# Plain fp32 gates in the first four pairs, row copies on ScalarE, and one-hot products inside a shared step, in a mixture-of-experts feed-forward kernel

## What is computed

```
y = einsum('bct,bcd->bdt', x, weights[conditions])        # 1024 tokens x 256
probs = softmax(y @ w_router); top_w, top_i = top_k(probs, 4)   # weights normalised to sum 1
g = silu(y @ we1[e]) * (y @ we3[e])                        # per chosen expert, hidden width 128
moe = sum over the four of top_w * (g @ we2[e])
shared = silu(y @ ws1) * (y @ ws3) @ ws2                   # hidden width 512
out = x + shared / 5 + moe * 4 / 5
```

## Time and profile before

| what | value |
|---|---|
| median of three runs | 180.62 us (178.18 to 182.24) |
| the profiled execution | 178.29 us |
| its span, first to last instruction | 176.5 us |
| mean granted TensorE clock | 0.934 of full speed |
| busy: TensorE, VectorE, ScalarE, GpSimd | 78%, 69%, 43%, 39% of the span |
| HBM read and written | 17.58 MB, 6.42 MB |

### The profile page before, as it was taken

The page is one execution under the profiler, slowest core; times in us unless marked ns, Lnnn a source line. Parts: engine busy times, 40 slices in busy tenths (PEclk is TensorE's granted clock), DMA queues, the critical chain, the costliest instruction groups (busy, mean ns, idle before and its releaser), DMA issues.

```text
span 176.5 us, 3102 instructions
## 1 busy us (share of the span) xinstructions
PE 137.0 (78%) x903; PEld 119.5 (68%) x903; DVE 122.0 (69%) x286; ACT 76.6 (43%) x168; POOL 69.0 (39%) x79
## 2 busy tenths in 40 slices
PE   5956979389862068739997999699999989697950
PEld 2416658178652058629987999699999978586930
DVE  3203688697889757843778786888887752677992
ACT  3004857945375055713483667464344411322000
POOL 1500000000677877777720055576766664200000
PEclk9999999979999558985899999999999999999996
DMA  3545889700399975697661235354453222289733
GB/s 93 184 102 127 248 260 298 240 4 0 85 266 303 335 213 146 185 281 227 163 184 61 92 135 195 119 194 166 179 207 127 91 90 88 45 257 385 300 106 132
DMA packets 29952, 30.50 MB, mean 173 GB/s; under 512 B 4688, under 2 KB 26832, under 8 KB 29936
## 3 DMA queue, kind: packets, MB, share of 16 engines
q1 hardware_dynamic: 22976, 19.41, 34.1%
q0 software_dynamic: 3120, 8.52, 14.9%
q10 hardware_dynamic: 3840, 2.38, 4.4%
HBM read 17.58 MB, written 6.42 MB: 136 GB/s over the span
## 4 chain that ended last, share of the span: by engine, by line
PE 49%; DVE 18%; DMA 10%; SPq 6%; ACT 6%; issue 6%; ACTq 2%; DVEq 1%
PE up_ps L927 17%; PE down_ps L945 9%; PE gate_ps L903 6%; PE gate_ps L854 5%; DVE acc L326 4%; DMA w_raw<-store_t 4%; PE up_ps L854 3%; DVE w_lo L577 3%; PE down_ps L869 3%; SPq L355 3%; PE down_ps L913 2%; DMA g<-in_L_cond_weights,cond_idx 2%; ACT g_hi L494 2%; DVE store_t L759 2%; DVE acc L722 2%
## 5 line engine op out<-in xcount | busy, mean ns | idle before, releaser
L419 POOL DMA_INDIRECT store_t<-y_of,token_i x32 | 35.0, 1094 | 47.4 <-DVE token_i L692 38.0
L426 POOL DMA_INDIRECT result<-store_t,back_i x32 | 31.1, 973 | 30.7 <-DVE store_t L759 26.1
L759 DVE SCALAR_TENSOR_TENSOR store_t<-down_ps,valid,store_t 128x256 f32 x47 | 22.7, 483 | 9.7 <-DVE store_t L759 5.2
L903 PE MATMUL gate_ps<-ident,w_raw 128*128 128x128 f32 x94 | 16.1, 299 | 12.0 <-DMA w_raw<-store_t 12.0
L903 PEld LDWEIGHTS gate_ps<-ident,w_raw 128*128 128x128 f32 x94 | 12.1, 154 | 12.8 <-issue 8.1
L522 ACT ACTIVATE g_hi<-down_ps 128x256 fp32r<-128x256 f32 (+1 forms) x24 | 9.1, 379 | 26.5 <-PE down_ps L913 26.5
L945 PE MATMUL down_ps<-w_hi,g_hi 128*128 x47 | 14.2, 303 | 5.0 <-DVE g_lo L735 5.0
L577 DVE TENSOR_TENSOR w_lo<-w_raw,w_hi 128x768 fp32r<-128x768 f32 x10 | 9.4, 953 | 10.0 <-ACT w_hi L453 9.9
L869 PE MATMUL down_ps<-w_hi,g_hi 128*128 128x256 f32 x32 | 9.5, 298 | 8.5 <-DVE g_lo L600 8.5
L530 ACT ACTIVATE sil<-up_ps 128x256 f32<-128x256 f32 (+1 forms) x24 | 9.1, 380 | 15.2 <-PE up_ps L927 15.2
L927 PE MATMUL up_ps<-w_hi,g_hi 128*128 x48 | 15.2, 316 | 0.0
(11 more groups left out here) (160 smaller groups left out, 369.5 us busy)
## 6 DMA issues: line engine op xcount, KB each, us to landing
w_raw<-store_t SPq DMA_DIRECT2D x48, 128.0 KB
w_lo<-result SPq DMA_DIRECT2D x8, 512.0 KB, 8.5
store_t<-in_L_ffn_we SPq DMA_DIRECT2D x30, 128.0 KB, 3.3
w_raw<-in_L_ffn_we SPq DMA_DIRECT2D x18, 128.0 KB, 3.6
w_raw<-in_L_ffn_ws SPq DMA_DIRECT2D x12, 128.0 KB, 2.7
acc<-in_x SPq DMA_DIRECT2D x2, 512.0 KB, 4.9
y_of<-store_t ACTq DMA_DIRECT2D x1, 1024.0 KB, 8.5
out<-acc ACTq DMA_DIRECT2D x8, 128.0 KB, 1.8
```

The source lines that it names most:

```text
L419: pool.indirect_dma_start(xs[:, j, :], None, y_of, bass.IndirectOffsetOnAxis(ap=token_i[:, j:j + 1], axis=0),).then_inc(tile_in[j % TT], 16)
L426: pool.indirect_dma_start(result, bass.IndirectOffsetOnAxis(ap=back_i[:, j:j + 1], axis=0), merged[:, j, :], None,).then_inc(result_out[j ...
L759: dve.scalar_tensor_tensor(out=into, in0=out_ps[n % 2][:, h, :], scalar=valid[:, it:it + 1], in1=into, op0=ALU.mult, op1=ALU.add).then_inc ...
L903: last = pe.transpose(xt_ps[b][:, h, k * P:(k + 1) * P], xt[:, r, h, k * P:(k + 1) * P], ident[:, :])
```

## The change

1. **Layouts.** Unit buffers hold gate and up only (128x512). All 13 early raw buffers stay resident, so loads wait for nothing up to the loop (SP goes from 178 rows to 28 in the program); down weights `w_2` come in bigger loads of their own and are used as plain fp32. Rows and weights are read in an order that makes pieces in DRAM twice as long.
2. **Down products in plain fp32** (shared and experts): one matmul in place of three, no high and low part of the gated product. ScalarE only copies the turned product (`gt`).
3. **Gates of pairs 0 to 3 in plain fp32** from the raw weights (`PLAIN = 4`): they need no split. From pair 4 on three fp32r matmuls per product as before.
4. **Row copies by ScalarE**, two pairs ahead (`AHEAD = 2`), no longer by DMAs of the SP queue. Gathers on GpSimd from the ninth on wait until TensorE has turned enough pairs (`LEAD = 6`).
5. **Router**: logits come out untransposed, 32 small matmuls in place of 8 large ones, a copy and 8 transposes.
6. **One-hot products** stand between the gate half and the up half of shared step 2; `row_hot` is made by 32 small VectorE instructions (`tensor_scalar`) in place of 4 large ones (`tensor_tensor`); the item table's arithmetic stands behind the products.
7. **Clearing**: 8 result tiles by ScalarE before the loop, the other 24 by VectorE memsets, two tiles each, in rounds 4 to 15.
8. **The end**: ScalarE weights the rows of tiles 0 to 3, VectorE adds them for two tiles at once, combines tiles 4 and 5 itself, and TensorE takes tiles 6 and 7. Stores go by two tiles on SP, the last on ScalarE's queue.

```diff
-    RAW = 4
+    PLAIN = 4
+    LEAD = 6
+    AHEAD = 2
-    SPLIT = {0: UNITS - 3, 1: UNITS - 2, 2: UNITS - 1, 6: UNITS, 12: UNITS + 1}
+    SPLIT = {0: [9, 10], 1: [11, 12], 2: [13], 3: [14], 7: [16], 9: [17], 12: [18], 14: [19]}
...
             for j in range(TILES):
...
+                if j >= LEAD + 2:
+                    pool.wait_ge(t_turned, (j - LEAD) // 2)
...
+            def copy_pair(n):
...
+                for i in range(halves(n)):
+                    j = 2 * n + i
+                    if j < TILES:
+                        act.wait_ge(tile_in[j % TT], 16 * (j // TT + 1))
+                    act.activation(xt[:, n % RING, i, :], xs[:, bass.ds(tiles[j], 1), :].rearrange("p a d -> p (a d)"), ACT.Copy).then_inc(xt_out, 1)
...
+            def rows_hot(c):
+                for n in range(TT * c, TT * c + TT):
+                    dve.tensor_scalar(row_hot[:, n, :], count_r[:, :], row_f[:, n:n + 1], None, ALU.is_equal).then_inc(row_hot_done, 1)
...
+                        if n < PLAIN:
+                            for k in range(KD):
+                                last = pe.matmul(gu_ps[b][:, h, :], x_f[b][:, h, k * P:(k + 1) * P], pair_of(raw, experts[h], k),
+                                                 start=(k == 0), stop=(k == KD - 1))
+                            continue
...
-                        for m, (a, w) in enumerate([(0, w_hi), (1, w_hi), (0, w_lo)]):
-                            last = pe.matmul(out_ps[b][:, h, :], tg[a][:, b, h, :], of(w, experts[2 + h], 2 * KD * H, WC),
-                                             start=(m == 0), stop=(m == 2))
+                        last = pe.matmul(out_ps[b][:, h, :], gt[:, b, h, :], w2_of(experts[2 + h]), start=True, stop=True)
...
+                if ZEROED <= i < TILES // 2:
+                    dve.wait_ge(xt_out, 2 * i + 2)
+                    dve.memset(merged[:, 2 * i:2 * i + 2, :], 0.0).then_inc(t_cleared, 1)
...
+            def gather_pair(t):
+                dve.wait_ge(weighted, 2 * TOP_K * (PAIR_TILES.index(t) + 1))
+                two = four[:, t:t + 2, :, :]
+                dve.tensor_tensor(two[:, :, 0:2, :], two[:, :, 0:2, :], two[:, :, 2:4, :], ALU.add).then_inc(combined[t], 1)
```

More of the change, by code:

```diff
@@ new lines, in _ @@
+            for c in range(1, TOP_K):
+                rows_hot(c)
+            gated(1)
+            dve.wait_ge(inverted, 1)
+            chain(dve.tensor_copy(token_f[:, :], dest_ps[:, 1, :]))
+            dve.scalar_tensor_tensor(out=token_i[:, :], in0=dest_ps[:, 0, :], scalar=float(TT), in1=token_f[:, :],
+                                     op0=ALU.mult, op1=ALU.add).then_inc(token_done, 1)
+            dve.wait_ge(token_done, 1)
+            dve.scalar_tensor_tensor(out=back_i[:, :], in0=token_i[:, :], scalar=float(TOP_K), in1=dest_ps[:, 2, :],
+                                     op0=ALU.mult, op1=ALU.add).then_inc(back_done, 1)
@@ L746, in _ @@
                 if i < 2:
-                    add_shared(i, STEPS - 1 + i)
-                if i in SPLIT:
-                    low(SPLIT[i])
+                    add_shared(i, STEPS // 2 * (i + 1))
+                for n in SPLIT.get(i, []):
+                    low(n)
+                if i == 10:
+                    weights()
+                if ZEROED <= i < TILES // 2:
+                    dve.wait_ge(xt_out, 2 * i + 2)
+                    dve.memset(merged[:, 2 * i:2 * i + 2, :], 0.0).then_inc(t_cleared, 1)
+                if i % 6 == 1 and (first := 2 * (i - 1)) < ITEMS_UP:
+                    registers = [dve.alloc_register(f"merge{first + n}") for n in range(12)]
+                    dve.wait_ge(items_done, 4)
+                    dve.load(registers, item_t_i[0:1, first:first + 12])
+                    tiles += [dve.snap(r, donate=True, min_val=0, max_val=TILES - 1) for r in registers]
                 if (n := pair_at(i, 2)) is not None:
@@ new lines, in combine @@
+            def combine(t):
+                dve.wait_ge(back[t], 16)
+                for k in range(TOP_K):
+                    if k:
+                        dve.wait_ge(combined[t], k)
+                    dve.scalar_tensor_tensor(out=acc[:, t, :], in0=back_in[t][:, k, :], scalar=top_w[:, t, k:k + 1], in1=acc[:, t, :],
+                                             op0=ALU.mult, op1=ALU.add).then_inc(combined[t], 1)
+            dve.wait_ge(added, 4)
+            for s in range(STEPS, LAST_STEP - 1):
+                gated(s)
@@ L888, in _, with turn_pair @@
-            down(STEPS - 1)
+            pe.wait_ge(back_done, 1)
+            pe.wait_ge(items_done, 4)
+            down(1, [1])
+            def turn_pair(n):
+                r, b = n % RING, n % 2
+                pe.wait_ge(xt_out, min(2 * n + 2, ITEMS))
+                if n < 2:
+                    pe.wait_ge(silu_done, STEPS - 1 + n)
+                for h in range(halves(n)):
+                    for k in range(KD):
+                        last = pe.transpose(xt_ps[b][:, h, k * P:(k + 1) * P], xt[:, r, h, k * P:(k + 1) * P], ident[:, :])
+                last.then_inc(t_turned, 1)
@@ L890, in load_experts @@
+            turn_pair(0)
+            down(3)
             def load_experts(at):
```

567 lines of the change are left out of this document (271 added, 296 removed).

## The result

| | before | after |
|---|---|---|
| median | 181.39 us (178.18 to 182.78, 6 runs) | 158.98 us (157.28 to 161.3, 6 runs) |
| the profiled execution, its span | 178.29, 176.5 us | 159.25, 157.3 us |
| mean granted TensorE clock | 0.934 | 0.974 |
| busy: TensorE, VectorE, ScalarE, GpSimd | 78%, 69%, 43%, 39% | 88%, 65%, 52%, 42% |

A forecast was written before the change was run, and what follows sets the result against it. TensorE was taken to bound the loop and VectorE the part ahead of it. Gains of 7.2 + 13.5 - 2.0 + 3.6 + 1.2 = 23.5 us off the 176.5 span gave 153.0, forecast as 155, range 147 to 166.

The forecast's parts named there:

- TensorE bounds the loop: Rounds 5 to 23: TensorE binds at 2.95 us a round, 59.6 us against 57.6 before, 2.0 lost.
- the four holds: Rounds 7, 9, 12 and 14: late splits delay the next gated product by 1.2, 1.0, 0.65 and 0.65, 3.5 us.
- The signs: Events that would show the forecast right, from the first row gather near 38 to the end 25 us behind the last merge.
- The token indices: Front, to the end of the indices' cast: at 36.9 us, 7.2 earlier, with TensorE late if `row_hot` is cheap.
- From the indices to pair 5: Stretch up to the turning of pair 5, following VectorE: 26.6 us in place of 40.1, 13.5 gained.
- Last rounds: From round 24 to the last merge: 4.4 us in place of 8.05, 3.6 gained.
- The end: From the last merge to the kernel's end: 25.3 us in place of 26.5, 1.2 gained.
- A: Rival in the loop: VectorE sets the round, 3.3 us each, 161 to 162 us; chance 0.17.
- B: Rival at the start: late loads, pairs 0 to 3 at 1.2 GHz, 160 to 164 us; chance 0.14.
- C: Rival, better than forecast: late splits hide and the clock stays, 148 to 150 us; chance 0.09.
- D: Rival, slower than before: row copies in ScalarE's queue wait for gathers in the loop, 180 to 190 us; chance 0.03.
- E: Rival, nothing net: time saved ahead turns up as a wait for the read back; chance 0.02.

The follow-up runs named there:

- Experiment 2: Changed kernel with low parts of tiles 16 to 19 made one round later: 156.97 us, ratio 0.8781; on a second, slower chip 175.39 us, 0.8507.
- experiment 3: Changed kernel with twelve warming products in place of eight ahead of the conditions' product: 158.66 us, ratio 0.8867 to the kernel before.
- experiment 4: Changed kernel with three unread filler products in TensorE's wait in round 2: 158.8 us, ratio 0.8799 to the kernel before.
- experiment 5: Changed kernel with no pair's gates in plain fp32, on two slower chips: 175.91 us (ratio 0.8491) and 179.32 us (0.8643).
- experiment 7: Changed kernel without the gathers' wait for turned pairs, on two slower chips: 195.89 us (ratio 0.9469) and 197.28 us (0.9382).

## Why the prediction was right, and where it was off

- **TensorE bounds the loop.** Right: busy 56.95 of 59.20, and pairs 5 to 23 took 59.4 us against 59.6. The round of 2.95 and the sum of the four holds, forecast 3.5 and measured 3.3, came from the right pieces. One by one they were mis-sized: forecast 1.2, 1.0, 0.65 and 0.65, measured 0.86, 0.73 and 0.17, 0.82 and 0.73 in the spacing of the turnings. Experiment 2 shows that the low parts' place causes two thirds of them. The fp32 down, named as the loss, takes 0.86 as forecast; undoing it in the changed kernel needs room for the high and low parts of these weights that its layout doesn't have, and it wasn't tried.
- **The signs.** All named events came, 2.5 to 4.3 us late: the first row gather at 40.5 (near 38), the first expert gate at 51.3 (near 48), pair 5 turned at 67.1 (by 64), the last merge over at 131.3 (near 127), and the end 26.1 us behind it (25).
- **The token indices: the step that failed.** Forecast at 36.9 for the end of their cast (7.2 is 44.1 less 36.9), measured 39.69, 2.8 us late of a forecast gain of 7.2. The term took the conditions' product over from before, at 3.8 us. It took 5.56, since TensorE stood still for 4.21 us ahead of it and was granted 0.72 in the window; experiment 3 takes the idle time away and gets 1.4 us back at the indices and at the end. In the kernel before, the product had run at the full clock after a gap of nearly the same length, in the timeline of its TensorE:

```profile
14.93 1.16 PE L792 MATMUL gate_ps<-store_t,acc 128*128 128x128 f32 x8 [3.61 <-DMA store_t<-cond_of]
15.92 1.06 PE L792 MATMUL up_ps<-store_t,acc 128*128 128x128 f32 x8
```

  So the duration was copied with its clock, while for the expert rounds had shown the price and it was used. That is 1.7 us. The product also starts 0.26 us later, and from its end to the slots it takes 9.2 us in place of 9.6, a gain of 0.4 where 0.6 was forecast. `row_hot` took 32 instructions in 5.39 us, 0.166 to 0.175 each against 0.15, 0.6 us in all, but the chain above passes only its first eight (1.40 us against 1.2) and then goes through TensorE: the shared down (1.97 us against 4 x 0.43) and the gate half. So TensorE is the late one there, as the prediction had it for a cheap `row_hot`. The Trainium skill (VectorE: DVE Perf Modes, the perf-mode tier table) would have `tensor_scalar` on bf16 run four elements a cycle, by which the prediction put it at 3.0 us, with a fixed part of 58 cycles; the trace does not agree with that price. It has one size only, so it does not show whether the rate or the fixed part is off.
- **From the indices to pair 5.** Forecast 26.6, measured 27.5 (39.69 to 67.14). The order of events was as told: the wait for the product of step 3, seven low parts (4.31 us), then rounds of 3.25. The clock was put at 1.5 us here, and experiment 4 measured 1.7. The other 0.7 lie in pieces too small to name.
- **Last rounds.** From 126.58 to 131.27 it took 4.7, forecast 4.4.
- **The end.** 26.0 us behind the last merge, forecast 25.3, so 0.5 of the forecast 1.2 is gained. The sums were over 23.3 us behind the merge for 22.8 forecast, with VectorE's combining at 142.12, 10.9 after the merge for 9.9. Part of it is that GpSimd is behind with its issues at 1.28 us each, the last at 132.53, and the read back waits for them, in the chain that ended last:

```profile
132.53 2.39 DMA result<-store_t,back_i
135.00 3.75 DMA raw<-result
```

  The read back starts 3.7 us behind the merge, before it was 3.3. No run tested this alone. In experiment 5's first trace GpSimd is not behind (last issue 0.4 us after the merge, read back at 2.8); the combining starts at 10.5 there and the end comes 25.8 us behind the merge, so this is worth about 0.3 us, and the rest stays open.
- **The rivals.** A, VectorE sets the round: out, 44.38 of 59.20. B, late loads: out, no load releases a gate, though its low clock in pairs 0 to 3 came in part. C: the clock of its 148 to 150 is what experiments 3 and 4 bring, 3.1 us together. D, ScalarE standing for gathers: on a chip of 180 us 1.4 us in all, in two places ahead of pair 3, none in the loop from pair 5 on. E: out.

Summed over the five terms: 2.8 + 0.9 - 0.2 + 0.3 + 0.7 = 4.5, against 4.3 between the two spans; the 0.2 are rounding in the prediction, whose stages add up to 152.8 and whose gains give 153.0. Experiment 3 accounts for 1.4 of it. Four of the five stages took longer than forecast; misses cancel only inside the loop, among the four holds.

## What to carry to other kernels

Before work is moved in time, ask of each idle stretch of TensorE what runs behind it, and price that at the low clock: in this kernel four more warming products in one gap and three in another are worth 1.4 and 1.7 us in their traces, and the prediction priced only the second, because the first had cost nothing in the kernel before. When one engine splits what another has just made, put it a round later, so that it doesn't wait in the middle of its queue. And a wait that paces GpSimd's gathers can be worth more than it seems to cost: some 18 us on one chip here, and 15 or more on another (0.9382 against the 0.8643 of experiment 5, whose own edit costs time); on a chip like that of the result it was not run without it.

## What was not expected of the hardware

- The kernel before takes 180 us on one chip and 206 and 208 on two others. There, with the gathers paced, ScalarE stands some 2 to 6 us at a time at several places, with releases the profile doesn't know. The turnings of pairs 12 and 14 are 10.3 to 14.5 us apart in these six traces, 6.1 in the changed kernel's. A stand of ScalarE of 2.6 to 6.0 us begins there, 0 to 1.4 us after GpSimd's first scatter, which follows its last gather at once, with the first five scatters 1.3 us apart. With the gathers unpaced the longest waits are 9 to 17 us, the last of them over at 85, 5 us behind the last gather's issue; the first scatters come 35 us later, and pairs 12 to 14 take 6.9. So neither that place of ScalarE's program nor the first scatters alone bring the stand: it came where gathers had just been issued as well. The changed kernel on the chip of the result has the same issues at the same spacing and no such wait. What holds ScalarE stays open; no run tested it. One candidate: the Trainium skill (Runtime: NRT & Kernel Launch, Instruction fetch mechanics) says that each engine fetches its instructions in blocks through a DMA queue of its own, and takes this to be mostly hidden. The profile does list two queues of the kind instruction, with 7 and 6 packets in the changed kernel. But in experiment 7's first trace no packet of either lies between 49 and 100 us, while three long waits of ScalarE end there, at 64, 74 and 85: no listed packet released them. Whether ScalarE's blocks come through one of the two listed queues is not shown.
- A lower clock with TensorE busy all the time, 0.72 from 21 to 33 us in the profiled execution of experiment 4, cost 3 us. Experiment 2's trace from the second chip has it too (0.63 from 21 to 27, 0.80 from 27 to 33, TensorE busy throughout). In both TensorE had been busy since 14.6 us and the clock back at 1.00 for 2 us or more, so idle time just ahead isn't needed. The mean clocks of the four long executions of experiment 4 would fit the same fall, but only one of them has a trace.
